# Reordering the prologue of an FFN, attention, FFN kernel: the first half's gate and up products, the down weights, and the picker rows

## What is computed

```python
x = x + 0.5 * ffn(layernorm(x), w_gate, w_up, w_down)
x = x + attn(layernorm(x), w_qkv, w_out, q_gain)
x = x + 0.5 * ffn(layernorm(x), w_gate, w_up, w_down)

def ffn(x, w_gate, w_up, w_down):     # 512 -> 2048 -> 512
    gate = einsum('bsd,hd->bsh', x, w_gate)
    up = einsum('bsd,hd->bsh', x, w_up)
    return einsum('bsh,dh->bsd', silu(gate) * up, w_down)
```

## Time and profile before

| | us |
|---|---|
| median of 3 runs (lowest, highest) | 2886.03 (2885.43, 2886.33) |
| the profiled execution | 2886.31 |
| its span, first to last instruction | 2884.6 |
| PE busy | 2760.6 (96%) |
| VectorE, ScalarE, GpSimd busy | 1773.9, 1193.5, 536.4 |
| mean granted clock of TensorE, of its full speed | 0.989 |
| start of the first gate product | 94.57 |
| start of attention's first transposes (L1108) | 238.63 |

### The profile page before, as it was taken

One profiled execution on the slowest core, in us unless ns is written; L12 is line 12 of the kernel. 1 busy time (PEld: TensorE's weight loads), 2 busy tenths in 40 slices (PEclk: granted clock), 3 DMA queues, 4 the chain that ended last, 5 costly groups with the idle time before them and its releaser, 6 DMA issues.

```text
span 2884.6 us, 56180 instructions
## 1 busy us (share of the span) xinstructions
PE 2760.6 (96%) x23232; PEld 2025.3 (70%) x23232; DVE 1773.9 (61%) x4156; ACT 1193.5 (41%) x2218; POOL 536.4 (19%) x820
## 2 busy tenths in 40 slices
PE   4699999999999999999999999999999999999999
PEld 4467776677677776777777777677777766777676
DVE  8655657565756565665655666565666657665643
ACT  5233444344533443344434444334443444344422
POOL 0103031303131211213012130212203031303100
PEclk8899999999999999999999999999999999999999
DMA  6000000000000000000000000000000000000000
GB/s 250 15 1 1 16 1 1 1 16 3 14 1 16 16 1 1 1 16 16 1 1 1 16 16 1 1 16 1 16 1 16 16 1 1 1 16 9 1 9 15
DMA packets 16574, 39.37 MB, mean 14 GB/s; under 512 B 1472, under 2 KB 1472, under 8 KB 15808
## 3 DMA queue, kind: packets, MB, share of 16 engines
q1 hardware_dynamic: 16320, 35.79, 3.5%
HBM read 26.35 MB, written 9.44 MB: 12 GB/s over the span
## 4 chain that ended last, share of the span: by engine, by line
PE 84%; DVE 11%; ACT 3%; issue 2%; POOL 1%; DMA 0%; SPq 0%; ACTq 0%; DVEq 0%
PE psum L1003 24%; PE psum L1005 24%; PE psum L1004 24%; PE psum L1153 2%; PE psum L1130 2%; DVE mneg L917 2%; PE psum L1165 1%; PE psum L1112 1%; PE psum L1046 1%; PE psum L1108 1%; DVE arena L865 1%; DVE arena L867 1%; DVE arena L938 1%; DVE arena L860 1%; PE psum L1131 1%
## 5 line engine op out<-in xcount | busy, mean ns | idle before, releaser
L1003 PE MATMUL psum<-arena,WG 128*128 128x256 f16 x2048 | 559.2, 273 | 1.4 <-DVE arena L860 1.4
L1005 PE MATMUL psum<-arena,WG 128*128 128x256 f16 x2048 | 559.3, 273 | 0.0
L1004 PE MATMUL psum<-arena,WG 128*128 128x256 f16 x2048 | 559.1, 273 | 0.0
L1003 PE MATMUL psum<-arena,WU 128*128 128x256 f16 x2048 | 558.7, 273 | 0.0
L1005 PE MATMUL psum<-arena,WU 128*128 128x256 f16 x2048 | 558.5, 273 | 0.0
L1004 PE MATMUL psum<-arena,WU 128*128 128x256 f16 x2048 | 558.5, 273 | 0.0
L865 DVE SCALAR_TENSOR_TENSOR arena<-arena,psum 128x256 f32<-128x256 f32 x512 | 215.1, 420 | 508.8 <-ACT arena L735 508.0
L735 ACT ACTIVATE arena<-psum,tscale 128x256 f32<-128x256 f32 x512 | 242.3, 473 | 661.1 <-PE psum L1005 660.9
L1003 PE MATMUL psum<-WD,arena 128*128 128x512 f16 x1024 | 388.6, 379 | 12.7 <-DVE arena L871 12.7
L1005 PE MATMUL psum<-WD,arena 128*128 128x512 f16 x1024 | 388.5, 379 | 0.0
L1004 PE MATMUL psum<-WD,arena 128*128 128x512 f16 x1024 | 388.4, 379 | 0.0
(11 more groups left out here) (139 smaller groups left out, 4534.8 us busy)
## 6 DMA issues: line engine op xcount, KB each, us to landing
arena<-in_L_attn_x SPq DMA_DIRECT2D x16, 512.0 KB, 3.7
out<-arena SPq DMA_DIRECT2D x16, 512.0 KB, 2.8
arena<-in_L_ffn_w_gate SPq DMA_DIRECT2D x4, 1024.0 KB, 9.3
arena<-in_L_ffn_w_up SPq DMA_DIRECT2D x4, 1024.0 KB, 9.3
WD<-in_L_ffn_w_down SPq DMA_DIRECT2D x4, 1024.0 KB, 11.6
arena<-in_L_attn_w_qkv SPq DMA_DIRECT2D x1, 3072.0 KB, 20.4
WQ<-in_L_attn_w_out SPq DMA_DIRECT2D x1, 1024.0 KB, 22.7
park<-arena SPq DMA_DIRECT2D x2, 512.0 KB, 2.8
```

The costliest lines, as they stand in the source:

```text
L1003: T_.matmul(o, lhs(0), rhs(0), start=first, stop=False)
L1004: T_.matmul(o, lhs(0), rhs(1), start=False, stop=False)
L1005: return T_.matmul(o, lhs(1), rhs(0), start=False, stop=last)
```

## The change

The first half's sixteen steps are put down as gate and up alone; their gated products are kept in two halves in SBUF (fourteen in a new view `far` over the not yet used `QT` and `KT`, two in the usual buffers), and fourteen down products follow in a row. From step 16 on the pieces are as before.

The down weights' preparation becomes stages of the list. "wd turn" and "wd out" (n = 0 to 15) stand behind pieces 1 to 16, one group of four transposes each, in the banks 0, 1, 2, 6, 7. The copy out of PSUM is ScalarE's and doesn't multiply. The maximum is taken per hidden channel in four parts (after groups 3, 7, 11, 15), the gate and up scales are multiplied into the 16 maxima and later into the 16 factors (`pgs`), and halves and remainders are made in sixteen parts of 512 columns behind pieces 20 to 35. `WD32` now lies in the buffers of the projection and output weights, the raw output weights in `xb`.

The first tokens are loaded behind up blocks 0 and 1, the four down loads behind the last up load, the output weights behind the eighth transposed block. Statistics, norms and the first turn stand before the last block's eviction. Tiles 2 and 3 are normalized from piece 24 on (2 before). Magnitudes stand at pieces 37 to 45, scales at 47, weights at 50 to 64. The picker rows come from ScalarE in four copies of a row of ones, scaled with a per-partition column (`pick`), at pieces 53, 55, 57, 59. The edits of `wait(...)` into `pe.wait_ge(...)` and the like are the same waits.

```diff
+    FAR = HC - 2
+    far = arena[:, place["qt"][0] + D:place["qt"][0] + D + FAR * TH].bitcast(F16).rearrange("p (j s n) -> p j s n", j=FAR, s=2)
+    def H2(j):
+        return [far[:, j, q] for q in range(2)] if j < FAR else HP[j % 2]
...
-        pieces = [piece for j in range(len(steps) + 2) for piece in ffn_units(j)]
+        pieces = []
+        for j in range(HC):
+            pieces += [[("gate", j)] + [("gated", j - 1)] * (j > 0), [("up", j)] + [("parts", j - 1)] * (j > 0)]
+        pieces += [[("down", 0), ("gated", HC - 1)], [("down", 1), ("parts", HC - 1)]] + [[("down", j)] for j in range(2, HC - 2)]
+        pieces += [piece for j in range(HC, len(steps) + 2) for piece in ffn_units(j)]
...
-        put(("stats", 0, 0, 0), ("stats", 0, 0, 1), ("norm", 0, 0, 0), ("turn", 0, 0, 0), ("norm", 0, 0, 1), ("split", 0, 0, 0),
-            ("turn", 0, 0, 1), ("split", 0, 0, 1))
-        normalize(2, 0, 0, (2, 3))
-        late = {4: ("magnitude", 0, 0), 5: ("magnitude", 0, 1), 6: ("magnitude", 0, 2), 7: ("magnitude", 0, 3), 8: ("magnitude", 1, 0),
-                10: ("scales", 0, 0), 11: ("pickers", 0, 0), 12: ("weights", 1, 0), 14: ("weights", 0, 0), 15: ("weights", 0, 1),
-                16: ("weights", 0, 2), 17: ("weights", 0, 3)}
+        put(("w scales", 0), ("w rows", 0), ("w scales", 1))
+        for j in range(8):
+            if j + 2 < 8:
+                put(("w scales", j + 2))
+            if j + 1 < 8:
+                put(("w rows", j + 1))
+            put(("w turn", j))
+            if j == 7:
+                put(("stats", 0, 0, 0), ("stats", 0, 0, 1), ("norm", 0, 0, 0), ("turn", 0, 0, 0), ("norm", 0, 0, 1))
+            put(("w out", j))
+        put(("split", 0, 0, 0), ("turn", 0, 0, 1), ("split", 0, 0, 1))
+        normalize(24, 0, 0, (2, 3))
+        late = {n + 1: [("wd turn", n), ("wd out", n)] + [("wd max", n // 4)] * (n % 4 == 3) for n in range(HC)}
+        late[19] = [("wd scales", 0)]
+        for k in range(HC):
+            late[20 + k] = [("wd parts", k)]
+        late.update({37 + 2 * k: [("magnitude", 0, k)] for k in range(KC)})
+        late.update({45: [("magnitude", 1, 0)], 47: [("scales", 0, 0)], 50: [("weights", 1, 0)]})
+        late.update({53 + 2 * g: [("pickers", g)] for g in range(GH)})
+        late.update({52 + 4 * k: [("weights", 0, k)] for k in range(KC)})
...
-                if j >= 4:
-                    t = j - 4
-                    sp.dma_start(RAWD[t], w_down[t * P:(t + 1) * P, :]).then_inc(s["down_in"], 16)
+                if j in (4, 5):
+                    th = j - 4
+                    sp.dma_start(xa[:, 2 * th:2 * th + 2, :], half_of(x[0], th)).then_inc(s[f"x_in{th}"], 16)
+            for t in range(4):
+                sp.dma_start(RAWD[t], w_down[t * P:(t + 1) * P, :]).then_inc(s["down_in"], 16)
...
+            sp.wait_ge(s["w_tr"], 8)
             sp.dma_start(RAWO.rearrange("p (k n) -> p k n", k=KC), w_out.rearrange("(k p) n -> p k n", p=P)).then_inc(s["out_in"], 16)
-            for th in range(2):
-                sp.dma_start(xa[:, 2 * th:2 * th + 2, :], half_of(x[0], th)).then_inc(s[f"x_in{th}"], 16)
-            sp.wait_ge(s["wd_lo"], 4)
+            sp.wait_ge(s["pro_lo"], 1)
             sp.wait_ge(s["xn_done"], TT)
...
-                link(nc.gpsimd.memset(kr, 4096.0))
...
+            def wd_out(m):
+                act.wait_ge(s["dn_tr"], m + 1)
+                q, t = m // 4, m % 4
+                nc.scalar.activation(WD32[q][:, :, t * P:(t + 1) * P], ps(wd_bank(m)).rearrange("p (k n) -> p k n", n=P), ACT.Copy).then_inc(s["dn_st"], 1)
+            def wd_parts(k):
+                act.wait_ge(s["scales"], 1)
+                nc.scalar.activation(WD[:, 0, k, :], WD32[k // 4][:, k % 4, :], ACT.Copy, scale=pgs[:, k:k + 1]).then_inc(s["wd_hi"], 1)
+            def pickers(g):
+                if g == 0:
+                    act.wait_ge(s["down_done"], FAR)
+                ones = halves("v", 0, S)[ST:ST + MR, :].rearrange("p (a n) -> p a n", a=2)
+                nc.scalar.activation(KT[ST:ST + MR, g::GH, :], ones, ACT.Copy, scale=pick[ST:ST + MR, g:g + 1]).then_inc(s["sel_done"], 1)
...
+            def wd_max(q):
+                dve.wait_ge(s["dn_st"], 4 * q + 4)
+                pro_link(V_.tensor_reduce(dmax[:, 4 * q:4 * q + 4], WD32[q], AX_X, ALU.max, apply_absolute_value=True))
+                if q == 3:
+                    pro_link(V_.tensor_tensor(pgs[:, :], dmax[:, :], pgu[:, :], ALU.mult))
+                    V_.tensor_reduce(gmax[:, 0:1], pgs[:, :], AX_X, ALU.max).then_inc(s["gmax_in"], 1)
+            def wd_parts(k):
+                dve.wait_ge(s["wd_hi"], k + 1)
+                V_.scalar_tensor_tensor(out=WD[:, 1, k, :], in0=WD32[k // 4][:, k % 4, :], scalar=pgs[:, k:k + 1], in1=WD[:, 0, k, :], op0=ALU.mult, op1=ALU.subtract).then_inc(s["wd_lo"], 1)
...
-            pe.wait_ge(s["wd_lo"], 4)
...
+                if m >= 5:
+                    pe.wait_ge(s["dn_st"], m - 4)
...
+                if j < HC:
+                    pe.wait_ge(s["wd_lo"], j + 1)
```

More of the change, by code:

```diff
@@ L559, in _ @@
             link(nc.gpsimd.memset(mhalf[:, :], -0.5))
+            rows = pick[ST:ST + MR, :]
+            link(nc.gpsimd.memset(rows, 4096.0))
+            link(nc.gpsimd.affine_select(out=rows, in_=rows, compare_op=ALU.is_ge, fill=0.0, base=0, pattern=[[-2, GH]], channel_multiplier=1))
+            link(nc.gpsimd.affine_select(out=rows, in_=rows, compare_op=ALU.is_ge, fill=0.0, base=1, pattern=[[2, GH]], channel_multiplier=-1))
             link(nc.gpsimd.memset(mst[:, :], 0.0))
@@ L645, in scale_rows, with w_out @@
                 ins.then_inc(s["wscaled"], 1)
-            scale_rows(0)
-            for j in range(8):
-                if j + 1 < 8:
-                    scale_rows(j + 1)
+            def w_out(j):
                 act.wait_ge(s["w_tr"], j + 1)
@@ L914, in row_max @@
             def row_max(b, hf, h, bank):
-                wait("s1_ps", 3 * head_no(b, hf, h) + bank + 1)
+                dve.wait_ge(s["s1_ps"], 3 * head_no(b, hf, h) + bank + 1)
                 for t in QBANKS[bank]:
@@ L990, in weights @@
                                         in1=W[:, 0].rearrange("p k n -> p (k n)"), op0=ALU.mult, op1=ALU.subtract).then_inc(s["pro_lo"], 1)
-            run({"magnitude": magnitude, "scales": scales, "weights": weights,
+            run({"w scales": w_scales, "w out": w_out, "wd max": wd_max, "wd scales": wd_scales, "wd parts": wd_parts, "magnitude": magnitude, "scales": scales, "weights": weights,
                  "stats": stats, "norm": norm, "split": split, "gated": gated, "parts": parts, "residual": residual,
@@ L1007, in _, with wait, take, turn @@
             pe.wait_ge(s["c_made"], 1)
-            for j in range(8):
+            def wait(name, k):
+                pe.wait_ge(s[name], k)
+            reader = {2: None, 3: ("w_lo", 28)}
+            scored = [None]
+            def take(bank, *last):
+                if reader[bank]:
+                    wait(*reader[bank])
+                reader[bank] = last
+            def turn(b, u, t):
+                k, bank = place_of_norm[b, u, t], 3
+                pe.wait_ge(s["xn_done"], k + 1)
+                take(bank, "xt_lo", k + 1)
+                for kc in range(KC):
+                    ins = T_.transpose(ps(bank, kc * P, P), xn[xn_of(b, u, t)][:, kc * P:(kc + 1) * P], ident[:, :])
+                ins.then_inc(s["xt_ps"], 1)
+            def w_turn(j):
                 pe.wait_ge(s["wscaled"], j + 1)
@@ L1016, in _, with wd_turn @@
                 ins.then_inc(s["w_tr"], 1)
[L1018 to L1020 removed]
+            def wd_turn(m):
                 q, t = m // 4, m % 4
[L1022 to L1023 removed]
+                if m == 0:
+                    pe.wait_ge(s["down_in"], 64)
+                    pe.wait_ge(s["w_lo"], 32)
+                if m >= 5:
+                    pe.wait_ge(s["dn_st"], m - 4)
                 for i in range(4):
[L1025 removed]
+                    ins = T_.transpose(ps(wd_bank(m), i * P, P), RAWD[t][:, (4 * q + i) * P:(4 * q + i + 1) * P], ident[:, :])
                 ins.then_inc(s["dn_tr"], 1)
[L1027 to L1047 removed]
             def half_product(j, W, at):
@@ L1060, in gate @@
                 if j >= 2:
-                    wait("gated", j - 1)
+                    pe.wait_ge(s["gated"], j - 1)
                 if i % HC == 0:
-                    wait("xt_lo", place_of_norm[b, 2 * f, 2 * (i // HC) + 1] + 1)
+                    pe.wait_ge(s["xt_lo"], place_of_norm[b, 2 * f, 2 * (i // HC) + 1] + 1)
                 half_product(j, WG, 0)
@@ L1195, in out_product @@
                     reader[2] = "x2_done", TT * b + 3
-            run({"turn": turn, "gate": gate, "up": up, "down": down, "qkv": qkv, "stack turn": stack_turn, "scores max": scores_max,
+            run({"w turn": w_turn, "wd turn": wd_turn, "turn": turn, "gate": gate, "up": up, "down": down, "qkv": qkv, "stack turn": stack_turn, "scores max": scores_max,
```

265 lines of the change are left out of this document (111 added, 154 removed).

## The result

The changed kernel takes 2853.85 us (median of 4 runs, 2853.28 to 2854.06) against 2886.18 before: 32.3 us faster, ratio 0.9888 with a 95% interval of 0.9871 to 0.9905. The forecast was 2852.6 us, 1.2 us less. On another chip, later, the same kernel took 2855.63 (2854.44 to 2856.90) against 2886.39, ratio 0.9894 (0.9879 to 0.9909), so a difference of one or two microseconds between runs of different chips says nothing.

The account below looks back on a forecast made before the run. TensorE, busy 96% of the span, was taken as the bound. Gain 34.7 - 6.9 + (16.7 - 10.8) = 33.7 us, so 2886.3 - 33.7 = 2852.6 us; forecast range 2847 to 2860 (0.74), wider range 2843 to 2867.

Parts of the forecast that it names:

- Step 1: First gate product, with token statistics and norms ahead of the last up block's eviction: at 59.9 us, gaining 34.7 us.
- Step 2: 64 down-weight transposes move in behind the first gate product: 0.107 us each, +6.9 us; waiting for their loads 0.
- Step 3: Gate and up without down: maxima cost TensorE 2 us, halves with tiles 2; projection maxima under down products 0.
- Step 4: Picker rows from GpSimd to ScalarE, pieces 53 to 59: the 9.55 us wait and 2.5 us of clock go.
- Step 5: Projection weights move from pieces 36 to 51 to pieces 50 to 64: down(17) 2 to 2.6 us late, 3.5 charged.
- small remainder: A term of 1 us among the new losses in the forecast's sum.
- Rival B: Clock stays at 0.50 throughout the 32 gate and up pieces and the transposes: +42 us, 2895 us; chance 0.05.
- A: VectorE and ScalarE set the pace of the first phase: some 11 to 13 us more, 2866 us; chance 0.12.
- D: Gain not kept: a later fixed-time wait, such as the next tokens' loads, costs 30 us: 2883 us; chance 0.03.

Follow-up runs that it names:

- the three moves: New kernel with maxima one piece later, tiles 2 and 3 normalized from piece 34, and qkv weights at pieces 62 to 71: 2848.48 us, ratio to before 0.9867.

## Why the prediction was right, step by step

**Step 1, the start.** Forecast 59.9 us, measured 60.19 (59.6 to 60.2 in the other traces). The chain was the one worked out: eviction of block 6 to 50.67 us (0.45 later than in the trace of before), statistics and norms 3.5 us, remainders, splits. -34.4 us against -34.7. The first tokens were there in time, as said.

**Step 2, the transposes.** 0.11 us each between the products, 6.9 us, and shown by doing them twice. That their data is there "by about 60" us, even one load after another, doesn't follow from the row: 27.81 + 4 x 11.6 = 74. It did no harm. The four loads were issued between 30.1 and 33.3 us and landed in a median of 12.3, and the first transposed block ran at 62.72 without a wait.

**Step 3, VectorE.** Maxima: four waits as said, but 0.43 three times and 1.59, 2.9 us instead of 2. The last is longer for two reasons, worked out and not tried: no transposed block follows it, so PE gets through the next gate and up product 2 x 0.44 us sooner; and two small instructions (L984, L985) stand behind the fourth maximum, so that the gated product starts 0.32 us after it ends and not 0.04. 0.43 + 0.88 + 0.28 = 1.59. Halves and tiles: 0.57 + 1.37 = 1.9 us, charged at 2. The down products hid the projections' maxima: PE was busy 20.00 of 20.00 us from 117 to 137. The remainder of 512 columns took 0.74 us, where I had 0.62; but the instruction behind it starts 0.66 us after it, so 0.66 is what one costs VectorE.

**Step 4, the pickers.** ScalarE's four copies took 1.14 us each (1.1 estimated), and no wait of PE is put down to them; the 9.55 us and the clock behind it went, shown by doing that part alone (-10.8) and by undoing it.

**Step 5, the projection weights.** down(17) waited 2.39 us ("2 to 2.6"), down(18) 0.37; 2.8 us instead of 3.5. The 1 us that the sum has for a "small remainder" has no working in the prediction, and no further wait stands in the stretch.

**The sum of the losses.** The waits in the stretch are 7.6 us and the half clock at its start 4.81 x 0.33 = 1.6 us. Each wait costs a little more than the idle time shown: four pieces take 7.59 us (72.82 to 80.41), of which 4 x 1.3 + 4 x 0.44 = 7.0 are work, so 0.6, not 0.43, is the wait. The kernel with later maxima bears this out: without waits four such pieces take 6.98 us there. With 0.17 more for each of eight (an estimate, since it was seen at one kind of wait) that is 7.6 + 1.4 + 1.6 = 10.6 us; 10.8 were charged. The sum came out closer than its parts, and that is luck: with this addition the maxima (3.6 against the 2 charged) and the halves with the tiles (2.3 against 2) were charged 1.9 us too low, and the clock (1.6 against 2.3), the projection weights (3.1 against 3.5) and the small remainder (0 against 1) 2.1 us too high.

**What was missing** is the third row of the table: 1.5 us in the 2650 us in which "nothing later moves but in time". Work and waits there are the same. The two waits at this place, in before and in after (timelines of PE), and the windows behind them:

```profile
746.91 0.61 PE L1153 MATMUL psum<-arena 104*128 104x384 f16 x3 [0.61 <-DVE mneg L917]
748.72 0.19 PE L1165 MATMUL psum<-arena 128*128 128x65 f16 x1 [1.19 <-DVE arena L860]
```
```profile
749.00:752.50 3.50, 3.50 (x45) 3.14 (x42) 3.34 (x8) 1.78 (x3) 0.28 (x1) 1.00 0.00 0
```
```profile
712.85 0.61 PE L1186 MATMUL psum<-arena 104*128 104x384 f16 x3 [0.61 <-DVE mneg L928]
714.65 0.19 PE L1198 MATMUL psum<-arena 128*128 128x65 f16 x1 [1.19 <-DVE arena L871]
```
```profile
715.00:718.50 3.50, 3.50 (x31) 2.57 (x27) 3.27 (x8) 1.36 (x2) 0.21 (x1) 0.55 0.00 0
```

The same two waits, 0.61 and 1.19 us; full clock behind them before, some 3.5 us of mostly half clock after, and 31 products instead of 45 done. Rival B's "against", that the small gaps did not lower the clock, was true of that trace only.

**The rivals.** A (VectorE sets the pace) did not happen; with the remainders done twice it would have cost 9.5 us, about half of it half clock. B (half clock throughout) did not: 1.00 in the windows from 65 us on. For the rule of the Trainium skill's page "TensorE: Matmul & The Clock Gate", Part 4: PE-mode transpose, that full clock doesn't engage for transposes, the trace disagrees again: 1.00 with a quarter of the work in transposes. The same page of the Trainium skill, section "A second HAM failure mode: psum-queue depth-cycling", has frequent small pauses between groups of products as a cause of a swinging clock. The 715 us stretch agrees with it, at a price of 1.5 us instead of B's 42; the same two waits in before, at full clock, and the windows from 65 us on, with a wait in every fourth piece, do not. D (a later wait eats the gain) did not: the waits from the first stack transpose on are the same to 0.1 us.

## What to carry to other kernels

When an engine is the bound in 38 of 40 slices, the gain lies in the first two: bring its first instruction forward, and feed the preparation that stood in front of it into the pieces behind, one part per piece. Then count the work of the engine that gets the preparation, and not only its sum: the maxima of 2.3 us made waits where VectorE was busy 20.5 of 30 us, and the tiles where it was full. A burst ahead of what the bound engine needs next becomes a wait, and moving the burst by one piece or ten removes most of it, as the three moves showed (waits of 7.6 us down to 2.3). Covering time is not enough: the work must also be able to start in it, which is why the earlier projection weights lost.

## What the hardware did that I had not expected

The clock fell to half behind pairs of waits that left it alone in another run of the same place: some 3.5 us at half clock, 1.0 to 1.5 us lost in the time from the first stack transpose to the end (2646.1 us without one, 2647.1 with the one at about 2355 us, 2647.6 with the one at about 715, 2648.7 with both). Before had none there; the new kernel had the one at 715 us in both its traces, the kernels with later tiles and with later weights had both, and the others one of the two. The 2.39 us wait at down(17) was followed by such a stretch in three traces (transposes twice, remainders twice, maxima one piece later) and not in the new kernel's two or in the one with later tiles; the waits of 3.8 us at gate 18 were followed by one in both traces that have them.

What decides between them is not settled by these runs. The traces that differ at one place come from programs shifted against each other by some microseconds, and the two of the new kernel, on two chips, agree; but the other executions of one program need not: those with the weights later have spans of 2848.8, 2848.9, 2849.2 and, in the profiled one, 2852.4 us. The first rise, too, came at 63.3 us in one trace and 65.3 in another. So a schedule change of this kernel can't be timed to better than a microsecond or two by its median alone; the waits in a trace are the finer measure.
